# Moving weight preparation to the start of a fused attention and expert block on one core

## The reference, cut to what matters

```python
# x: 32 sequences x 256 tokens x 128 features, fp32
def layer(x):
    x = x + attention(layernorm(x))      # 16 heads of 8, causal window of 128 keys, softmax, projections
    x = x + experts(layernorm(x))        # 16 experts, hidden 64, plus one shared expert
    return x

def experts(x):
    scores = sigmoid(x @ gate_w.T)       # router; choice = scores + e_bias
    # the best 2 of 4 groups by the sum of their two best, then the best 4 experts, weights normalised, x 2.5
    inter = silu(x @ gate_proj[e].T) * (x @ up_proj[e].T)
    y = sum_e weight[e] * (inter @ down_proj[e].T)
    return y + shared_expert(x)
```

## Time and profile before

| | us |
|---|---|
| median of 3 runs | 761.21 |
| lowest, highest | 756.61, 762.22 |
| profiled execution, its own time | 758.62 |
| its span in the trace | 756.8 |
| mean granted TensorE clock | 0.972 |

### The profile page before, as it was taken

One profiled execution on the slowest core, in us unless ns is written; L12 is line 12 of the kernel. 1 busy time (PEld: TensorE's weight loads), 2 busy tenths in 40 slices (PEclk: granted clock), 3 DMA queues, 4 the chain that ended last, 5 costly groups with the idle time before them and its releaser, 6 DMA issues.

```text
span 756.8 us, 21746 instructions
## 1 busy us (share of the span) xinstructions
PE 706.9 (93%) x8499; PEld 472.2 (62%) x8499; DVE 585.8 (77%) x1741; ACT 362.4 (48%) x739; POOL 306.4 (40%) x327
## 2 busy tenths in 40 slices
PE   4597999999999999999778999999999999999997
PEld 2365666666666666666555666666666666666664
DVE  6776788888888888888577878887777888777632
ACT  2165566767776676667562332333333233333321
POOL 6410221222211222122215656566666656664543
PEclk9589899999999999999999999999999999999999
DMA  2125123333323222333118366654445666544550
GB/s 59 58 87 148 62 85 102 102 102 102 101 61 101 86 70 93 102 102 101 59 35 207 73 138 154 155 134 113 118 122 137 152 155 120 131 103 108 119 139 29
DMA packets 64837, 79.96 MB, mean 106 GB/s; under 512 B 10960, under 2 KB 38880, under 8 KB 64736
## 3 DMA queue, kind: packets, MB, share of 16 engines
q1 hardware_dynamic: 64736, 78.58, 39.9%
HBM read 61.00 MB, written 17.56 MB: 104 GB/s over the span
## 4 chain that ended last, share of the span: by engine, by line
PE 80%; DVE 7%; DMA 5%; ACT 4%; issue 2%; SPq 1%; POOL 1%; DVEq 0%; ACTq 0%; PEldq 0%
PE ps_c L1571 14%; PE ps_att L1356 7%; PE ps_sc L1330 6%; PE ps_max L1288 5%; PE ps_max L1560 4%; PE ps_max L1562 4%; PE ps_max L1561 4%; PE ps_sc L1306 4%; PE ps_sc L1561 4%; PE ps_sc L1562 4%; PE ps_sc L1560 4%; PE ps_a L1254 3%; ACT probs L683 3%; PE ps_c L1574 2%; PE ps_b L1247 2%
## 5 line engine op out<-in xcount | busy, mean ns | idle before, releaser
L618 POOL TENSOR_TENSOR probs<-probs,stacks 128x512 f32<-128x512 f32 x128 | 165.0, 1290 | 125.7 <-DVE probs L1105 75.4
L775 ACT ACTIVATE probs<-ps_max 128x512 f32<-128x512 f32 x144 | 86.2, 598 | 220.1 <-PE ps_max L1562 216.5
L886 DVE TENSOR_REDUCE chunkmax<-ps_max 128x16 f32<-128x512 f32 (+1 forms) x256 | 155.3, 648 | 37.9 <-PE ps_max L1269 37.8
L683 ACT ACTIVATE probs<-ps_sc 128x512 f32<-128x512 f32 x256 | 138.9, 595 | 48.6 <-PE ps_sc L1306 47.6
L1105 DVE TENSOR_TENSOR probs<-probs,ps_sc 128x512 f32<-128x512 f32 x128 | 87.3, 682 | 69.6 <-PE ps_sc L1562 26.4
L1571 PE MATMUL ps_c<-probs,wd 128*128 128x512 f32 x256 | 130.3, 592 | 1.3 <-POOL probs L618 1.3
L1560 PE MATMUL ps_max<-xh,whigh 128*128 128x512 f32 x144 | 93.7, 650 | 2.9 <-DVE probs L1105 2.1
L531 POOL TENSOR_TENSOR xres<-xin,cvec 128x512 f32<-128x512 f32 x16 | 20.6, 1287 | 141.1 <-DVE x L938 140.7
L1330 PE MATMUL ps_sc<-stacks 32*64 32x192 f16 (+2 forms) x2048 | 64.4, 232 | 9.5 <-ACT probs L683 2.7
L1356 PE MATMUL ps_att<-probs,stacks 128*32 128x192 f32 (+1 forms) x1536 | 70.2, 317 | 0.0
L1288 PE MATMUL ps_max<-hl,qdiag 32*128 32x160 f16 (+4 forms) x1024 | 50.9, 220 | 16.0 <-DVE chunkmax L886 9.7
(11 more groups left out here) (164 smaller groups left out, 1257.1 us busy)
## 6 DMA issues: line engine op xcount, KB each, us to landing
stacks<-weight_scratch SPq DMA_DIRECT2D x32, 1024.0 KB, 10.0
stacks<-qk_scratch SPq DMA_DIRECT2D x48, 256.0 KB, 3.4
qk_scratch<-hl SPq DMA_DIRECT2D x32, 256.0 KB, 3.4
xin<-in_L_attn_x_dram SPq DMA_DIRECT2D x16, 256.0 KB, 3.1
x_scratch<-x SPq DMA_DIRECT2D x16, 256.0 KB, 2.2
xin<-x_scratch SPq DMA_DIRECT2D x16, 256.0 KB, 8.9
xres<-x_scratch SPq DMA_DIRECT2D x16, 256.0 KB, 8.9
out_dram<-result SPq DMA_DIRECT2D x16, 256.0 KB, 8.8
```

The costliest lines, as they stand in the source:

```text
L618: nc.gpsimd.tensor_tensor(inter[p % 3], gated[p % 2], spread[d % 2][:, p, :], ALU.mult).then_inc(inter_ready, 1)
L683: nc.scalar.activation(dst[:, :], ps_sc[s][:, 0:dst.shape[1]], ACT.Exp, scale=SCALE).then_inc(probs_ready, 1)
L775: nc.scalar.activation(silu[n % 2][rows, :], ps_max[n % 2][rows, :], ACT.Silu).then_inc(silu_ready, 1)
L886: nc.vector.tensor_reduce(chunkmax[:, 2 * pair + m, at:at + CHUNKS[h]], ps_max[m][:, 0:BANK_COLS[h]].rearrange("p (n k) -> p n k", k=KB), ...
```

## The change

- SP issues `load_ffn_weights` at once after the first loads, with three semaphores. A new `copy_stacks` copies the filled rows of `qkstack` set 0 to set 1 by a DMA.
- GpSimd's `clear` is gone. ScalarE copies `vdiag` set 0 to set 1 (`copy_vdiag`).
- Block 0 is normalised by VectorE (`first_normalise`), between its filling of `qkstack` and of `vdiag`. GpSimd makes only the reciprocal deviation.
- The first maxima u = 1, 3, 5 of block 0 go to `ps_b` and `ps_c`, so that four banks are used.
- The weights (9 banks now) are transposed among those maxima, into `ps_sc`; ScalarE copies each twice, and GpSimd makes the low part (`low_weights`). TensorE waits for all of them before `body(1)`.
- In the turn no weight is left. Block 16 (block 0 of the experts) is transposed in `body(15)`. Blocks 17 and 18 are transposed in `last`, and so is the routing weight of block 0. The last half of attention block 15 and the routing of block 1 move among the first `up`s, with new orders for VectorE (`first_block`), ScalarE and GpSimd.

```diff
@@ sync @@
             sp.dma_start(bv[:, :], b_in[2 * P:3 * P].unsqueeze(1)).then_inc(b_loaded, 16)
+            sp.dma_start(boB[:, :], b_out.partition_broadcast(P)).then_inc(bo_loaded, 16)
             sp.dma_start(xin[1][:, :, :], x_t[1]).then_inc(x_loaded[1], 16)
-            sp.dma_start(boB[:, :], b_out.partition_broadcast(P)).then_inc(bo_loaded, 16)
...
+            def copy_stacks():
+                sp.wait_ge(buffers_ready[0], 1)
+                sp.dma_start(qkstack[1][3:P:4, :, :, :].rearrange("q n g t -> q (n g t)"),
+                             qkstack[0][3:P:4, :, :, :].rearrange("q n g t -> q (n g t)")).then_inc(stacks_copied, 16)
...
+            load_ffn_weights()
+            copy_stacks()
             for i in BODIES:
...
+                if i == 0:
+                    sp.wait_ge(stacks_copied, 16)
                 load_max(i, 0)
-                if i == 1:
-                    load_ffn_weights()
@@ gpsimd @@
-            layer_norm(0)
+            inverse_deviation(0)
+            pool.wait_ge(pool_chain, 2)
+            pool.sem_inc(rstd_ready, 1)
+            pool.sem_inc(pool_chain, 1)
...
+            def low_weights():
+                for n in SPLIT:
+                    dst, _ = WEIGHT_BANKS[n]
+                    pool.wait_ge(fw_high, n + 1)
+                    nc.gpsimd.tensor_tensor(low_of(dst), turned_of(dst), high_of(dst).bitcast(FP32),
+                                            ALU.subtract).then_inc(fw_low, 1)
             for i in range(STEPS):
                 residual(i)
                 if i == 0:
-                    clear()
+                    other_constants()
                 layer_norm(i + 1)
                 if i == 0:
-                    other_constants()
+                    ffn_constants()
+                    low_weights()
@@ scalar @@
+            def first():
+                high_part(0, 0)
+                high_part(0, 1)
+                copy_vdiag()
+                take_weight(0)
+                act.wait_ge(buffers_ready[1], 1)
+                spread_v(0)
+                take_weight(1)
+                take_weight(2)
+                transpose_out(1)
+                for n in range(3, len(WEIGHT_BANKS)):
+                    take_weight(n)
@@ scalar, last @@
                 exps(now, 3)
+                high_x(1)
                 exps(now, 4)
-                take_weight(2)
+                scores_of_experts(0)
                 exps(now, 5)
+                high_x(2)
                 take_att(now, 0)
...
                 exps(now, 9)
-                take_weight(7)
+                take_weights(0)
                 take_att(now, 1)
@@ vector @@
             statistics(0)
-            clear()
+            clear_stacks()
+            first_normalise()
+            clear_values()
...
             def last(now):
+                low_x(0)
                 normalise(now - 1, 1)
                 chunk_maxima(now, 7)
                 row_maxima(now, 1)
                 add_residual(now - 1, 1)
...
                 statistics(STEPS + 2)
+                low_x(1)
+                choices(0)
+                sum_pairs(0)
                 normalise(now, 0)
+                low_x(2)
+                for stage in (sum_groups, compare_groups, count_wins, mask_groups, find_best, mark_best):
+                    stage(0)
                 choose_experts(0)
                 shares(0)
+                add_residual(now, 0)
...
+            def first_block():
+                gate(0, 0)
+                normalise(STEPS - 1, 1)
+                sum_logits(1)
+                clip(1)
+                invert(1)
+                gate(0, 1)
+                choices(1)
+                sum_pairs(1)
+                sum_groups(1)
+                gate(0, 2)
+                add_residual(STEPS - 1, 1)
+                compare_groups(1)
+                count_wins(1)
+                gate(0, 3)
+                mask_groups(1)
+                find_best(1)
+                mark_best(1)
+                gate(0, 4)
+                choose_experts(1)
+                shares(1)
+                statistics(STEPS + 3)
+                gate(0, 5)
+                sum_logits(2)
+                clip(2)
+                invert(2)
+                gate(0, 6)
+                choices(2)
+                sum_pairs(2)
+                sum_groups(2)
+                gate(0, 7)
+                compare_groups(2)
+                count_wins(2)
+                mask_groups(2)
+                gate_shared(0)
+                find_best(2)
+                mark_best(2)
+                choose_experts(2)
+                shares(2)
@@ tensor @@
+            def first():
+                project_qk(0, 0)
+                project_qk(0, 1)
+                project_v(0, 0)
+                project_v(0, 1)
+                pe.wait_ge(consts_ready, 1)
+                score_maxima(0, 0)
+                project_v(0, 2)
+                project_v(0, 3)
+                score_maxima(0, 1)
+                transpose_weight(0)
+                score_maxima(0, 2)
+                transpose_weight(1)
+                score_maxima(0, 3)
+                transpose_weight(2)
+                transpose_x(1)
+                score_maxima(0, 4)
+                transpose_weight(3)
+                score_maxima(0, 5)
+                transpose_weight(4)
+                score_maxima(0, 6)
+                for n in range(5, len(WEIGHT_BANKS)):
+                    transpose_weight(n)
...
                 scores(now, 2)
-                pe.wait_ge(ffn_loaded, 16 * 8)
-                pe.wait_ge(max_free, 16 * STEPS)
-                transpose_x1(0)
-                transpose_weight(0)
-                transpose_weight(1)
+                route(0)
+                transpose_x(STEPS + 1)
                 scores(now, 3)
...
                 scores(now, 9)
-                transpose_weight(7)
+                transpose_weights(0)
                 attend(now, 1, 1)
                 attend_tails(now, 1)
-                transpose_weight(8)
...
-                project_att(now, 1)
+            first()
+            pe.wait_ge(fw_high, len(WEIGHT_BANKS))
...
+                    if d == 0 and p == 0:
+                        transpose_att(STEPS - 1, 1)
+                        route(1)
+                    if d == 0 and p == 1:
+                        transpose_attn(STEPS - 1, 1)
+                    if d == 0 and p == 2:
+                        project_att(STEPS - 1, 1)
-                    if p == 1:
+                    if p == (5 if d == 0 else 1):
                         route(d + 2)
```

More of the change, by code:

```diff
@@ L207, in build_block @@
         ffn_consts_ready = sem("ffn_consts_ready")
-        cleared = [sem(f"cleared{p}") for p in range(2)]
+        cleared = sem("cleared")
+        stacks_copied = sem("stacks_copied")
         wt_done = sem("wt_done")
@@ L252, in build_block @@
         nd_chain = sem("nd_chain")
-        ffn_loaded = sem("ffn_loaded")
+        ffn_loaded = [sem(f"ffn_loaded{n}") for n in range(3)]
         fw_done = sem("fw_done")
@@ L950, in clear, with first_normalise @@
                 last.then_inc(buffers_ready[0], 1)
+            def first_normalise():
+                dve.wait_ge(rstd_ready, 1)
+                for t in range(NT):
+                    last = nc.vector.tensor_scalar(xhat[:, t, :], xin[0][:, t, :], meanvar[:, t, 0:1], rstd[:, t:t + 1],
+                                                   ALU.subtract, ALU.mult)
+                last.then_inc(xhat_ready, 1)
             def body(i):
@@ L1431, in _, with transpose_weight @@
             mm(ps_att[:, 0:E], bvB[:, :], wT[:, 3, :], start=True, stop=True).then_inc(cvec_done, 1)
+            def transpose_weight(n):
+                what, bank = WEIGHT_BANKS[n][0], ps_sc[n % 2]
+                loads = LOADED_BY[what[0]]
+                pe.wait_ge(ffn_loaded[0], 16 * 2)
+                if loads >= 3:
+                    pe.wait_ge(ffn_loaded[1], 16)
+                if loads >= 8:
+                    pe.wait_ge(ffn_loaded[2], 16 * 5)
+                after(pe, fw_high, n - 1)
+                if what[0] == "gu":
+                    for t in range(4):
+                        last = nc.tensor.transpose(bank[:, t * P:(t + 1) * P], wgu_raw[:, what[1] + t, :], ident[:, :])
+                elif what[0] == "sh":
+                    last = nc.tensor.transpose(bank[:, 0:P], wsh_raw[:, :], ident[:, :])
+                elif what[0] == "router":
+                    last = nc.tensor.transpose(bank[:, 0:NE], wr_raw[:, :], ident[0:NE, 0:NE])
+                elif what[0] == "down":
+                    for t in range(4):
+                        n2 = 2 * (what[1] + t)
+                        last = nc.tensor.transpose(bank[:, t * P:(t + 1) * P],
+                                                   wd_raw[:, n2:n2 + 2, :].rearrange("p e i -> p (e i)"), ident[:, :])
+                else:
+                    last = nc.tensor.transpose(bank[0:I, 0:E], wds_raw[:, :], ident[:, :])
```

(24 more changed lines are left out.)

289 lines of the change are left out of this document (114 added, 175 removed).

## The result

| | kernel before | changed kernel |
|---|---|---|
| median, us (runs) | 762.27 (7) | 766.96 (7) |
| lowest, highest | 756.61, 764.88 | 764.14, 772.52 |
| profiled execution, its span | 758.62, 756.8 | 765.52, 763.8 |
| mean granted clock | 0.972 | 0.967 |

What follows compares the result with a forecast made beforehand. TensorE, 93% busy, was taken as the bound, with gains only where it idles or runs at low clock. -3.3 - 1.7 - 6.1 + 5.5 = -5.6 us gave 753.0 profiled, 755.6 median; range 748.5 to 764.

Steps and rivals of the forecast that it cites:

- the prologue: Before body(1): without memsets beside spread_q, first scores start at 32.0 instead of 35.3 us; -3.3 us, bounds -5.0 to -1.0.
- the load: Step 1: expert weight load moved out, so its 27.1 us become 21.0; -6.1 us, bounds -4 and -6.1.
- the clock in the first body: body(1): TensorE's clock should be up by its start; -1.7 us, bounds 0 and -2.7.
- the turn: From attention to expert blocks: later landing plus VectorE's new work behind it; +5.5 us, bounds +2.6 and +10.
- TensorE's wait for block 17: Turn, ahead of scores(15, 3): TensorE idles 9 us where it idled 2.9, then resumes at the low clock.
- The landing: Turn: first spread issued 3.6 us later but taking 10.4 us instead of 12.4, so it lands 1.6 us later.
- 5.7 us of VectorE's work: Turn, behind the landing: residual 0.4, second half of routing 1 4.0, statistics of block 19 1.3; slack of 2.0 us subtracted.
- rival A: Turn nearly free, VectorE's backlog absorbed by its idle waits: turn costs 0 to 2.6 us, total about 751; chance 0.22.
- Contention with GpSimd: Turn: added two-input VectorE instructions held up by weigh; turn about 8 us if all met one, about 4 if none.
- Rival C: Turn's chain from block 17 to weigh: landing 5 us later, VectorE's 5.7 stretched to 10; +13, total 763; chance 0.10.
- B: Prologue: clock and weight banks hold body(1) to 35 us, first body stays cold; total about 760.5 us; chance 0.09.
- D: Prologue: moved loads jam SP, block 0's split store waits; at most 3 of 6.1 us lost, 758.6 us; chance 0.09.

Runs made afterwards that it cites:

- Experiments 6 and 8: The former: kernel before plus 65 unused semaphore increments starting TensorE's queue, ratio 1.0102; the latter: changed kernel plus 48 in TensorE's idle places, 0.9962.
- 9 and 10: Changed kernel, block 17 loaded early and transposed behind attend_tails(15, 0), routing of block 1 ahead of gate(0, 2): 0.9915; with 48 TensorE increments added: 0.9809.
- the 191 increments: Changed kernel plus 191 unused semaphore increments at the start of TensorE's queue: ratio 1.0378 to the kernel before.
- experiments 1 and 6: The former: kernel before with expert weight loads issued ahead of the body loop, ratio 0.9943; the latter: kernel before plus 65 TensorE increments, 1.0102.
- experiments 2 to 4: Changed kernel with block 17 transposed behind attend_tails(15, 0), 1.0001; with block 17 loaded earlier on SP, 0.9993; with both, 0.9943 (ratios to kernel before).
- Experiment 5: Changed kernel with the rest of block 1's routing, last residual and block 19's statistics moved on VectorE ahead of gate(0, 2): ratio 1.0010 to kernel before.

## Why the prediction was wrong

**Right: the prologue and the load.** `spread_q`, the row maxima at 24, the wait for `transpose_x(1)`, the scores at 32.0 and the 21.05 us of body 2 came as worked out. Up to the mark of body 1 the gain is 3.3 us and in body 2 6.1, both as forecast. The gain at the mark of body 4 is 9.8 us against 11.1; of the rest, 0.6 is the clock below and 0.6 is body 3 (21.62 us), with a late store. SP was free at 15.7 and not at 12 to 13, and its first split store went at 16.32 (15.80 before); the row maxima were not held up by it.

**Off: the clock in the first body, -1.1 us instead of -1.7.** I wrote that the clock should be up by `body(1)`. Windows of the changed kernel:

```profile
24.00:32.00 8.00, 7.00 (x59) 4.88 (x59) 3.87 (x7) 3.68 (x10) 6.14 (x10) 0.50 0.05 16
32.00:38.00 6.00, 5.97 (x68) 3.04 (x68) 2.13 (x10) 2.74 (x5) 1.05 (x1) 0.50 0.02 1
38.00:42.00 4.00, 4.00 (x72) 2.30 (x71) 3.40 (x8) 2.87 (x6) 0.00 (x0) 1.00 0.42 129
```

From 24 to 38 us the granted clock was half, with TensorE busy 7.00 of 8 and 5.97 of 6 us; it came back at 38, 6 us after the first scores, as it had come back at 42, 6.7 us after them. TensorE's wait of 3.8 us ahead of `transpose_x(1)`, which I had in the sum, is where it fell, at 21.0, 0.9 us into the wait. (In the kernel before it fell at 18.2, 2.9 us behind the last matmul, and not at 19 behind 3.6 us.)

**Wrong: "The steady bodies and expert blocks keep their order and cost nothing."** They kept their order and cost 4.8 us. I had not asked what else moves with moved code: the places at which TensorE's instructions are cut into blocks of 16 KB. The traces have 321 records of TensorE ahead of the first scores where the kernel before has 256, which is 65 more, and 895 in a body, or 3.5 blocks of 256; so the block that meets the store comes in every second body. Experiments 6 and 8 show it from both sides, 9 and 10 once more. The Trainium skill, Advanced Engine Details and Errata, section ISA Cache, states cache lines of 16 KB with 256 instructions each. The traces agree: 68 packets of 16 KB for TensorE's 17,485 records, and 69 with the 191 increments (17,676).

**Wrong: the turn, +11.9 instead of +5.5**, in this pair of traces past the upper bound of +10. Against the turns of experiments 1 and 6, whose code there is that of the kernel before (368.1 and 367.2), it is +8.4 and +9.3. So the forecast was too low by 3 to 6 us. By its terms:
- TensorE's wait for block 17 (9 us, was 9.77) and the spread's issue (+3.6, was +3.8) were right, and experiments 2 to 4 show that the wait is what makes the spread late.
- The landing was taken as 10.4 us because three transfers of 256 KB now come later. (The share given for it, 2.0 of 2.75 MB, would make 9.0 of the 12.4 us; the 10.4 has no working.) It took 12.38, as before (12.40): with the later issue +3.8 instead of +1.6. The three transfers had not been what makes it slow.
- Behind the landing I counted 5.7 us of VectorE's work less 2.0 of slack, and 0.2: 3.9. It was 7.7. The work was sized rightly; its place decided. Most of the routing of block 1 stands behind `gate(0, 2)`, and so behind the landing, while VectorE idles 7.68 us ahead of it; and its user, the second spread, is then late itself (4.77 us). I named rival A's idle time and never asked who waits for the routing's result. Experiment 5 took 7.3 us back by order alone.
- The clock had no term, though the text said that TensorE resumes at the low one. It was low for 27.3 us of the turn and for 10.2 before, with TensorE busy 13.1 and 8.7 us in it. As an estimate from these numbers, the 4.3 us more at half the clock are worth some 2 us. No experiment separates them from the waits that brought them.
- Contention with GpSimd was real (the needles' copy 1.09 us against 0.17) but no large part, since the same instructions fit ahead of the landing in experiment 5.
- 0.6 us of the turn is the late store of body 15, which belongs to the item above.

Rival C named the right chain and came near with +13, but by luck: it wanted a landing 5 us later (it was 3.8) and VectorE's 5.7 us stretched to 10 by GpSimd, and experiment 5 shows that their place cost them, not their length. With the gain of 9.8 the turn of this trace alone would have left the kernel 2 us slower. A fell with the turn, B with the first scores at 32.0, and D with the marks of body 2 and the row maxima at 24.

What stays open: why the landing of the first spread takes 12.4 us (12.2 to 13.2 in all these kernels; a single load of a spread takes 9.7 in the median), why blocks that start 1.3 to 1.7 us behind the issue hold up 11 stores of 47 and not the others, and why single bodies are long without a late store of row maxima. The traces have a hint that no run tests. The loads behind the split stores (`qk_scratch`) follow a median 4.0 us after the second of them; the only five that took over 5.1 in a steady body belong to bodies of 21.56 to 23.48 us (body 14 of the kernel before is one), each with a block 1.2 to 2.4 us behind that store's issue.

## What to carry to other kernels

When work is moved in the most heavily filled queue, everything behind it moves in the code as well. If bodies that were not touched get longer, look in windows of 0.25 us for 16 KB that no DMA of the program explains, beside the small transfers on which the next step waits; some increments in a place where the engine waits anyway are a cheap test, once their own cost is known. Ask the trace for every stretch also how long the clock was low. For work moved behind a wait, price two things: the idle time ahead of that wait, which it no longer uses, and the one who waits for its result.

## What was not expected of the hardware

- A block of 16 KB of instructions whose transfer starts 0.05 to 1.15 us behind the issue of an 8 KB store delays the load behind it from 1.4 us to between 2.1 and 3.5 (65 of 67 stores at 2.2 or more). At 1.3 to 1.7 us it did so in 11 of 47, up to 3.9.
- Increments of a semaphore in TensorE's queue stood 0.151 us apart (48, 65 and 191 of them).
- The first spread of 2 MB took 12.4 us with and without three transfers of 256 KB beside it.
